# Residual, mixing product and output projection of a graph layer moved into its edge loop, with accumulating scatters

## What is computed

```python
xn = layernorm(x)
q, k, v = xn @ Wq.T + bq, xn @ Wk.T + bk, xn @ Wv.T + bv      # 8 heads of 32
agg = segment_softmax_sum(q[dst], k[src], v[src], dst)        # one row per node
gnn = agg @ Wo.T + bo
mix = (q2 @ (instnorm(k2).T @ instnorm(v2) / N)) @ w_out.T + b_out   # linear in xn: xn @ M + b_out
x = x + gnn + mix
h = layernorm(x)
e = argmax(softmax(h @ gate_w + gate_b)); pos = rank of the node within its expert
x = x + prob * (relu(h @ w1[e] + b1[e]) @ w2[e] + b2[e]) if pos < 977 else x
```

## Time and profile before

| | |
|---|---|
| median of 3 runs | 3967.86 us (3959.5 to 3975.31) |
| the profiled execution | 3931.11 us |
| its span, first to last instruction | 3929.7 us |
| busy: PE, DVE, ACT, POOL | 59%, 68%, 16%, 53% |
| edge loop, first L1058 to last L1095 | 770.9 to 3245.5 us |
| node phase | to 3497.85 us |
| experts | to the end |

### The profile page before, as it was taken

One profiled execution on the slowest core, in us unless ns is written; L12 is line 12 of the kernel. 1 busy time (PEld: TensorE's weight loads), 2 busy tenths in 40 slices (PEclk: granted clock), 3 DMA queues, 4 the chain that ended last, 5 costly groups with the idle time before them and its releaser, 6 DMA issues. The chain is left out here.

```text
span 3929.7 us, 39441 instructions
## 1 busy us (share of the span) xinstructions
PE 2313.6 (59%) x9047; PEld 1778.6 (45%) x9047; DVE 2679.2 (68%) x3530; ACT 628.1 (16%) x1537; POOL 2065.1 (53%) x2048
## 2 busy tenths in 40 slices
PE   6568533745555454555555555555555558758988
PEld 3335422534433333434344333333434446658887
DVE  7386322677776776777778767677778775557776
ACT  7002211300000000000000000000000001224433
POOL 0410474266666666666665666666666654334443
PEclk9778766877777777777778777777777788779999
DMA  5314013266666666666666666666666647442221
GB/s 191 129 74 196 2 41 88 63 176 181 176 185 183 183 179 182 179 176 177 173 173 173 172 181 188 176 183 180 171 178 178 172 123 253 132 151 97 93 74 43
DMA packets 254845, 591.96 MB, mean 151 GB/s; under 512 B 78094, under 2 KB 119223, under 8 KB 252120
## 3 DMA queue, kind: packets, MB, share of 16 engines
q0 software_dynamic: 147472, 471.32, 43.2%
q1 hardware_dynamic: 104614, 113.05, 8.6%
q10 hardware_dynamic: 2240, 3.01, 0.2%
HBM read 513.32 MB, written 78.64 MB: 151 GB/s over the span
## 5 line engine op out<-in xcount | busy, mean ns | idle before, releaser
L875 POOL DMA_INDIRECT wide<-kv_d,arena x1099 | 1050.3, 956 | 669.6 <-issue 652.3
L955 PE MATMUL ps<-wide,arena 128*128 128x264 f32 x2432 | 802.0, 500 | 723.3 <-DVE wide L1077 393.9
L955 PEld LDWEIGHTS ps<-wide,arena 128*128 128x128 f32 x2432 | 601.4, 254 | 926.5 <-DVE wide L1077 427.9
L875 POOL DMA_INDIRECT arena<-kv_d,arena x539 | 515.4, 956 | 334.2 <-issue 313.8
L955 PE MATMUL ps<-arena 128*128 128x264 f32 x1216 | 390.6, 489 | 328.9 <-DVE arena L1077 174.4
L1065 DVE TENSOR_REDUCE ps<-arena 128x64 f32<-128x2048 f32 x228 | 523.2, 2295 | 7.9
L955 PEld LDWEIGHTS ps<-arena 128*128 128x128 f32 x1216 | 293.4, 248 | 427.4 <-DVE arena L1077 190.5
L1058 DVE TENSOR_TENSOR arena<-wide,ps 128x2048 f32<-128x2048 f32 x152 | 347.8, 2288 | 131.8 <-issue 131.8
L129 PE MATMUL ps<-halves 128*128 128x256 f32 (+2 forms) x2304 | 380.1, 328 | 35.4 <-DVE halves L1431 30.0
L1079 DVE TENSOR_TENSOR arena<-ps,arena 128x264 f32<-128x264 f32 x228 | 98.1, 430 | 407.7 <-remote 407.6
L129 PEld LDWEIGHTS ps<-halves 128*128 128x128 f32 x2304 | 345.1, 200 | 66.5 <-DVE halves L1431 33.2
(11 more groups left out here) (271 smaller groups left out, 2848.8 us busy)
## 6 DMA issues: line engine op xcount, KB each, us to landing
wide<-kv_d,arena POOLq DMA_INDIRECT x1099
hb_d<-arena SPq DMA_DIRECT2D x16, 1028.0 KB, 17.8
arena<-hb_d SPq DMA_DIRECT2D x16, 1028.0 KB, 7.6
arena<-in_w SPq DMA_DIRECT2D x16, 1024.0 KB, 5.0
kv_d<-wide SPq DMA_DIRECT2D x49, 260.0 KB
wide<-in_x SPq DMA_DIRECT2D x10, 896.0 KB, 6.0
arena<-kv_d,arena POOLq DMA_INDIRECT x539
q_d<-wide SPq DMA_DIRECT2D x49, 128.0 KB
```

The costliest lines, as they stand in the source:

```text
L875: e.indirect_dma_start(out=kvb[k][:, j, :], out_offset=None, in_=kv_d, in_offset=bass.IndirectOffsetOnAxis(ap=ixb[k][:, j:j + 1], axis=0)) ...
L955: e.matmul(psE[b % 2][:, 0:264], ident, kvb[b][:, j, 256:ROW], start=(j == 0), stop=False)
```

## The change

What moves into the loop, and what becomes of the node phase:
- A base row x + xn @ M + bo + b_out of every node is stored in x2_d. The last tile's base is made ahead of chunk 0, the other 48 in the first 48 chunks (AUX = 8 rounds of 6), one per chunk: SP loads the tile of xn_d and of x, TensorE makes five products into ps[4], ACT copies them over the loaded tile and stores it.
- At the end of a tile VectorE writes the mean to mo; TensorE transposes it, ACT copies it, TensorE multiplies with Wo, ACT copies the result over the tile's q.
- POOL, behind its last gather, adds all 49 tiles to x2_d with scatters that accumulate.
- The node phase loads x2_d into XH and makes the statistics of a whole group ahead of its tiles; centering is on ACT; turn_h and gate have three buffers; split_w(0, 0) comes first.
- xn_d has one row of 256 per partition and tile.

The loop's head, which all engines share, and SP:

```diff
         def rounds(e, pre, body):
             e.reg_load(cnt_, nch[0:1, 60:61])
+            e.reg_add(cnt_, cnt_, -AUX)
+            with e.Fori(0, AUX):
+                for k in range(RING):
+                    body(k, True)
             with e.Fori(0, val(e, cnt_)):
                 for k in range(RING):
-                    body(k)
+                    body(k, False)
...
+            def tile_in(k):
+                e.dma_start(xm[k], xn_d[bass.ds(val(e, u, 47 * 128), 128), :]).then_inc(e_x[k], 16)
+                e.dma_start(xr[k], x[bass.ds(val(e, u, 47 * 128), 128), :]).then_inc(e_x[k], 16)
+                e.reg_add(u, u, 128)
+            for k in range(RING):
+                indices(k)
+            e.wait_ge(sv.h, t_M[1])
+            e.wait_ge(s_xn.h, s_xn.n)
+            for k in range(RING):
+                tile_in(k)
+            e.dma_start(xm[RING], xn_d[48 * 128:NP, :]).then_inc(e_x[RING], 16)
...
+            with e.Fori(0, AUX - 1):
+                e.reg_add(bs, bs, 16)
+                for k in range(RING):
+                    indices(k)
+                    e.wait_ge(e_bs[k], bs)
+                    tile_in(k)
```

POOL behind its rounds, and ACT:

```diff
-            e.wait_ge(e_fin, NS)
-            for c in range(NS):
-                e.indirect_dma_start(out=agg_d, out_offset=bass.IndirectOffsetOnAxis(ap=permS[:, c:c + 1], axis=0),
-                                     in_=qs[:, c, :], in_offset=None).then_inc(s_ag.h, 16)
+            for k in range(RING):
+                e.wait_ge(e_bs[k], 16 * AUX)
+            e.wait_ge(e_bs[RING], 16)
+            for c in range(NT):
+                e.wait_ge(e_ao, c + 1)
+                e.indirect_dma_start(out=x2_d, out_offset=bass.IndirectOffsetOnAxis(ap=permS[:, c:c + 1], axis=0),
+                                     in_=qs[:, c, :], in_offset=None, compute_op=ALU.add).then_inc(s_ag.h, 16)
...
                 with e.If(val(e, last) > 0):
                     slow_tile(e, "a_", tf, ns, one)
                     e.reg_add(tf, tf, 1)
+                    weights()
+                    e.wait_ge(e_tp, tp)
+                    e.activation(aT, r3(ps[6][:, 0:256], 128), ACT.Copy).then_inc(e_at, 1)
+                    e.wait_ge(e_wo, fc)
+                    e.activation(qsf[:, bass.ds(val(e, o_at, NT * 256), 256)], ps[7][:, 0:256], ACT.Copy).then_inc(e_ao, 1)
+                with e.Else():
+                    weights()
+                if aux:
+                    e.wait_ge(e_bp, bc)
+                    e.activation(xm[k], ps[4][:, 0:256], ACT.Copy).then_inc(e_bc, 1)
+                    e.wait_ge(e_bc, bc)
+                    e.dma_start(x2_d[bass.ds(val(e, u, 47 * 128), 128), :], xm[k]).then_inc(e_bs[k], 16)
```

(`weights` is L938 to L940.) TensorE, behind L957, and VectorE's L1027:

```diff
+            def base_of(k):
+                o = ps[4][:, 0:256]
+                e.matmul(o, ident, xr[k], start=True, stop=False)
+                for i in range(2):
+                    e.matmul(o, xm3[k][:, i, :], M[:, i, :], start=False, stop=False)
+                e.matmul(o, ones[0:1, :], brow[:, 0:256], start=False, stop=False)
+                e.matmul(o, ones[0:1, :], brow[:, 256:512], start=False, stop=True).then_inc(e_bp, 1)
+            e.wait_ge(e_br, 32)
+            e.wait_ge(e_x[RING], 32)
+            base_of(RING)
...
+                tick()
+                with e.If(val(e, last) > 0):
+                    e.wait_ge(e_fin, fc)
+                    e.transpose(ps[6][:, 0:128], mo[:, 0:128], ident)
+                    e.transpose(ps[6][:, 128:256], mo[:, 128:256], ident).then_inc(e_tp, 1)
+                    e.wait_ge(e_at, fc)
+                    e.matmul(ps[7][:, 0:256], aT[:, 0, :], wo_s[:, 0, :], start=True, stop=False)
+                    e.matmul(ps[7][:, 0:256], aT[:, 1, :], wo_s[:, 1, :], start=False, stop=True).then_inc(e_wo, 1)
+                if aux:
+                    e.wait_ge(e_x[k], xw)
+                    e.wait_ge(e_bc, bp)
+                    base_of(k)
...
-                    e.tensor_tensor(q_old, sums_[:, :, 0:32], rin.unsqueeze(2).to_broadcast([128, 8, 32]), ALU.mult).then_inc(e_fin, 1)
+                    e.wait_ge(e_tp, tf)
+                    e.tensor_tensor(mo.rearrange("p (h d) -> p h d", d=32), sums_[:, :, 0:32], rin.unsqueeze(2).to_broadcast([128, 8, 32]), ALU.mult).then_inc(e_fin, 1)
```

The node phase (the loads of xres, xn_d and agg_d, the products with M, turn_a and project are gone):

```diff
+        wait(Y, t_fin, t_ag)
+        for grp in range(7):
+            t_x2[grp] = dma(Y, XH[:, grp * 7:grp * 7 + 7, 0:256], x2_d[grp * 896:(grp + 1) * 896, :].rearrange("(t p) d -> p t d", p=128), s_x2[grp])
...
+        def spread2(grp):
+            wait(V, t_x2[grp], t_h.get(grp * 7 - 8))
+            for i in range(7):
+                last = v(V.bn_stats(s2[:, 6 * i:6 * i + 6], XH[:, grp * 7 + i, 0:256]))
...
+            return a(S.activation(r, r, ACT.Sqrt))
...
         def center_h(u):
-            t_h[u] = v(V.tensor_scalar(out=XH[:, u, 256:512], in0=XH[:, u, 0:256], scalar1=mvs[b][:, 2 * i:2 * i + 1],
-                                       scalar2=rss[b][:, i:i + 1], op0=ALU.subtract, op1=ALU.mult))
+            t_h[u] = a(S.activation(XH[:, u, 256:512], XH[:, u, 0:256], ACT.Identity, bias=nms[b][:, i:i + 1], scale=rss[b][:, i:i + 1]))
...
+        load_w(0, 0)
+        split_w(0, 0)
+        t_nm = {0: scale2(0, spread2(0))}
+        for s_ in range(NT + 3):
+            grp, i = divmod(s_, 7)
+            if i == 0 and grp < 7:
+                t_o = out_group(grp)
+                if grp + 1 < 7:
+                    t_sq_ = spread2(grp + 1)
+                wait(S, t_nm[grp])
...
             if s_ < NT:
+                center_h(s_)
             if 0 <= s_ - 1 < NT:
+                turn_h(s_ - 1)
+            if 0 <= s_ - 2 < NT:
+                u = s_ - 2
                 gate(u)
...
+            if i == 1 and grp + 1 < 7:
+                t_nm[grp + 1] = scale2(grp + 1, t_sq_)
```

More of the change, by code:

```diff
@@ L105, in gps_layer_kernel @@
         src_d = dram("src_d", [NBP, 128], i32)
-        xn_d = dram("xn_d", [7 * 128, 1792])
+        xn_d = dram("xn_d", [NP, D])
         tab_d = dram("tab_d", [NP, 4], i32)
-        agg_d = dram("agg_d", [NP, D])
+        x2_d = dram("x2_d", [NP, D])
         hb_d = dram("hb_d", [H * CP, HR])
@@ L784, in gps_layer_kernel @@
             ("prod", "red", "mask", "max", "sw", "n0", "n1", "n2", "n3")]
-        e_fin = esem("fin")
+        e_fin, e_tp, e_at, e_wo, e_ao = [esem(n) for n in ("fin", "tp", "at", "wo", "ao")]
+        e_x, e_bs = [[esem(f"{n}{i}") for i in range(RING + 1)] for n in ("x", "bs")]
+        e_bp, e_bc, e_br, e_xz = [esem(n) for n in ("bp", "bc", "br", "xz")]
         s_ag = sem("s_ag")
@@ L1168, in gps_layer_kernel @@
+        s_x2 = [sem(f"s_x2_{i}") for i in range(7)]
+        wait(Y, t_fin, t_ag)
+        t_x2 = {}
+        for grp in range(7):
+            t_x2[grp] = dma(Y, XH[:, grp * 7:grp * 7 + 7, 0:256], x2_d[grp * 896:(grp + 1) * 896, :].rearrange("(t p) d -> p t d", p=128), s_x2[grp])
+        wait(V, t_fin)
         e3 = lambda ap: r3(ap, 8)
@@ L1183, in turn_h @@
         def turn_h(u):
-            pt = ps[5 + u % 2]
-            wait(T, t_h[u], t_hT.get(u - 2))
+            pt = ps[4 + u % 3]
+            wait(T, t_h[u], t_hT.get(u - 3))
             for k in range(2):
@@ L1188, in turn_h @@
             t_ = sp.inc(m)
-            wait(S, t_, t_lg.get(u - 2))
-            t_hT[u] = a(S.activation(hT[u % 2], r3(pt[:, 0:256], 128), ACT.Copy))
+            wait(S, t_, t_lg.get(u - 3))
+            t_hT[u] = a(S.activation(hT[u % 3], r3(pt[:, 0:256], 128), ACT.Copy))
         def gate(u):
@@ L1288, in group_end @@
[L1288 to L1297 removed]
+        nms = [R3[:, 4449 + 7 * i:4456 + 7 * i] for i in range(2)]
@@ L1298, in group_end @@
+        st2 = [st, R3[:, 3072:3072 + 42]]
+        def spread2(grp):
+            s2, mv2 = st2[grp % 2], mvs[grp % 2]
+            wait(V, t_x2[grp], t_h.get(grp * 7 - 8))
+            for i in range(7):
+                last = v(V.bn_stats(s2[:, 6 * i:6 * i + 6], XH[:, grp * 7 + i, 0:256]))
+            wait(V, last)
+            for i in range(7):
+                v(V.bn_aggr(mv2[:, 2 * i:2 * i + 2], s2[:, 6 * i:6 * i + 6]))
             r = rss[grp % 2]
             wait(V, (sv, sv.n))
-            last = v(V.tensor_scalar(out=r, in0=r3(mvs[grp % 2], 2)[:, :, 1], scalar1=EPS, scalar2=None, op0=ALU.add))
+            last = v(V.tensor_scalar(out=r, in0=r3(mv2, 2)[:, :, 1], scalar1=EPS, scalar2=None, op0=ALU.add))
```

190 lines of the change are left out of this document (68 added, 122 removed).

## The result

The changed kernel takes 4028.9 us (median of 4 runs, 4013.4 to 4033.7) against 3965.3 for the kernel before: the ratio of the means is 1.0151, 95% interval 1.0115 to 1.0187. I had forecast 3882. Slower by 1.5% where faster by 2% was expected. The profiled execution has a span of 4012.2 us, 82.5 more than the one of before.

A forecast was written before the change was run, and what follows sets the result against it. In the loop TensorE had no room at the low clock, VectorE and POOL some; terms -98 (node phase), +6 (before the loop), +3.5 (loop head), +2.5 (tile ends) gave -86, from 3967.9 to 3882 us, range 3785 to 3965.

The forecast's parts named there:

- I take both as cancelling: 0: In the loop, TensorE's added base and tile-end work and the higher clock from filled gaps were to cancel: 0 us.
- the third rival: In the loop, added work keeps TensorE's clock up and its waits shrink: 150 us less, 3732 in all; chance 0.15.
- The first rival: In the 48 base chunks TensorE becomes the bound, seen at L1079's wait: +173 us, 4055 in all; chance 0.10.
- The node phase: From the loop's end to the first expert matmul: 154.5 us instead of 252.4, so -98.
- Start of the scatters: After the loop's gathers: POOL's last gather ends at 3196.0 and the 49 scatters begin 1.3 us later.
- Pitch: In the node phase: accumulating scatters start 1.28 us apart, the same as plain ones.
- the rival of the dear scatter: In the node phase, scatters with addition cost far more than plain ones: +89 us, 3971 in all; chance 0.10.
- From the last scatter to the load: In the node phase: the first load of x2_d is issued 1.5 us after the last scatter's end.
- 49 tiles: In the node phase: 93 us from first tile to last logits, at 1.17 us a tile plus statistics and routing batches.
- Last routing to the first expert: At the node phase's end: a routing batch of 7.0 us, then an unchanged 23.5 us to the first expert matmul.
- POOL's split: Moved to the node phase's start, it was charged nothing; without cover it would cost 6.4 us again.
- Before the loop: TensorE's base of the last tile ahead of chunk 0 and ACT's delayed first q copy: +6 us, ends 0 and 12.

The follow-up runs named there:

- the third pair: Profiles of the kernel before and the unedited changed kernel, on one chip and one occasion; ratio 1.0159, with the kernel before at 3928 us.
- the first pair: The first profiles of the kernel before and the changed kernel, of different occasions; the changed one's span is 4012.2 us, 82.5 more.
- the first group: Four edits of the changed kernel's loop, run together on one chip where the kernel before took 3305 us; ratios 0.9855 to 0.9959.
- copies_later: Changed kernel with ACT's tile-end and base copies one chunk later, behind that chunk's q copy; 0.9955 of the kernel before, which took 3305 us.
- stages_later: Changed kernel with ACT's copies and TensorE's tile-end stages spread over later chunks; 1.0072 of the kernel before, which took 3977 us.
- plain_scatter: Changed kernel with scatters that overwrite instead of adding; 1.0149 of the kernel before, which took 3934 us.
- no_base: Changed kernel without the bases of the first 48 tiles and with plain scatters; 0.9858 of the kernel before, which took 3305 us.
- the three pairs: Three sets of profiles of the kernel before and the unedited changed kernel; ratios 1.0151, 1.0134 and 1.0159.
- copies_later2: Changed kernel with ACT's copies a chunk later, run again on a slower chip; 1.0077 of the kernel before, which took 3977 us.
- after_again: The changed kernel run again, unedited; 1.0134 of the kernel before, which took 3934 us.
- no_gathers: Changed kernel without the gathers and index loads of the last 180 chunks; 0.8961 of the kernel before, which took 3976 us.

## Why the prediction was wrong

**The step that failed is "I take both as cancelling: 0".** The base products and the tile ends were to fill TensorE's idle gaps and be repaid by the clock. Measured in the third pair: +70 us in the base chunks, 1.5 each, and +25 in the rest. The clock repaid next to nothing: in the 48 chunks it went from 0.76 or 0.77 to 0.78 (0.80 in the first pair). TensorE's waits for VectorE stay: 465.4 us before the products of one group of the 180 chunks. The rule of the Trainium skill (TensorE: Matmul & The Clock Gate, "Why this matters for your kernels") that steadier work keeps the clock up did not bear the third rival out here, as the gaps were not closed.

**The deeper error is in reading "TensorE late" as load or clock.** I had seen that one wait was 8.66 us behind a burst of 5.51, called a late signal "dear", and gave it no price. The 407.6 us of waits were the mark of a chip on which TensorE's signals come late beside the gathers: such waits are zero where the gathers are away, and on the chip of the first group. The [1.97 <-issue] before that burst was no pause either: it starts 0.05 us behind the end of L1077. The change added three signals of TensorE per tile or chunk (base, transposes, product with Wo) that other engines wait for. Where they stood in front of the q copy they cost some 28 us, which copies_later gets back. By what steps the rest comes, of the base's products and loads and of the tile ends, isn't shown: stages_later takes the waits out of the tile ends and wins nothing.

**The first rival had the right engine, the wrong place and too high a price.** I placed it at L1079's successor, +3.6 a chunk; that wait fell to 15 us and 123 us more appeared at L1156 instead, behind ACT, whose new order I had described and priced at nothing. The rival's point of no gain, 1.8 us per base chunk, was not reached, and the kernel is slower all the same, because the other side of the sum was a third of what I had. "Slower" had a chance of 0.09, far too low. The range's lower end, 3785, also takes 97 of the clock's 150 us, more than the half that the text says.

**The node phase**, -98 forecast, -31 measured. Term by term, from the loop's end:
- Start of the scatters: 15.4 us later than I had it. The row gave 16.49 us of idle before L912 and I took them off, as if POOL were free. It still goes through the last chunks' waits for TensorE's signals (15.58 again here, 5.0 in copies_later on the first group's chip).
- Pitch 1.84 to 1.85 for 1.28: +27.6. This is the rival of the dear scatter at a third of its upper end. plain_scatter and no_base show that the addition makes it.
- From the last scatter to the load 7.1 us, not 1.5: +5.6. It is the end of the loop's block, which now comes behind the scatters; the last one had landed 4.8 us before the load, and with plain scatters the wait is 8.7.
- First load 5.65 us (5.2), statistics to the first turn 7.8 (9.8).
- 49 tiles in 113 us, not 93: the tile pace of 1.17 us was right, but two stretches between logits beside a routing batch's scatters to hb_d took 18.0 and 26.5 us, where copies_later on the first group's chip has 10.6 and 13.4. There ACT waits up to 9.9 us for the transposes, and there not. On that chip the 49 tiles take 92.5 us, as forecast: these 20 us, too, belong to the kind of chip.
- Last routing to the first expert: 30.5 us, as forecast. Whether POOL's split is free beside the statistics wasn't put to the test: of its time, 3448.6 to 3455.1, only the last 0.3 us lie beside one. Beside it VectorE's L1336 took 0.61 us, at other times 0.17.

Sum: 15.4 + 27.6 + 5.6 + 0.5 - 2.0 + 20 = 67, and -98 + 67 = -31.

**Before the loop**, +6 forecast: +11, -2 and -6 in the three pairs, no difference that can be told.

**The profile and the median.** The profiled execution of before lay 37 us under its median, as I said, and that of after 16 under its own. By medians the change is +64 us: about 95 in the loop less 31 in the node phase.

## What to carry to other kernels

Work that fits into an engine's idle time by the sum of durations still has a price if its result is waited for in order: ask what stands behind each new wait on every engine it passes, and price it with the longest answer seen, not the mean. An idle time put down to "remote" or "issue" isn't free room: compare its end with the ends of what the engine needs, and look for what makes it, for it may grow with the work put there. Where one engine sets the pace of a loop with no wait of its own, as POOL does on the first group's chip, added work on the others can be free; where it waits, it is not. An operation moved behind a new kind of transfer should be measured alone before the sum is built on it, and a change that trades stages should be timed on more than one chip.

## What the runs showed of the hardware

- The same kernel takes 3305 us on one chip and 3928 to 3977 on others, at the same 1.26 us per gather. Of the 715 us between copies_later and copies_later2, one kernel on two chips, 481 are in the loop, 213 ahead of it, 20 in the node phase and 1 in the experts. In the loop the difference is in TensorE's signals: on the first chip none is late; on the others about half of them come over 1 us behind the end of their instruction, up to 17 us (91 of 179, 634 us in all, in 180 chunks). Ahead of the loop 14 of 268 are late there, by 105 us in all (after_again), and none in copies_later.
- These late signals vanish with the gathers (no_gathers). The Trainium skill (SBUF — State Buffer, "Who interferes with whom") has TensorE never waiting for another user of the memory. The runs agree as far as they go: TensorE's products start 0.05 us (median) behind the VectorE instruction that they wait for, and it is the signals that are late. By what path, and why not on every chip, stays open; gathers of fewer bytes at the same pace were not tried. All times here are of recorded executions, and the record loses semaphore updates where the signals are late (597 of VectorE's 1427), so a part of the recording itself isn't excluded.
- 49 plain scatters in a row beside the last chunks lengthen the loop's end by 39 to 44 us on such chips, accumulating ones at a pitch of 1.85 us don't.
- A scatter with addition costs POOL 1.54 us, a plain one 0.97, for the same 128 rows of 1 KB.
